# Preparation of queries and keys placed six sixteenths of a tile earlier in every engine's order

## The reference, cut to what matters

```python
def xattn(q, k, v):            # 8 heads of 32 rows each, softmax over the 512 columns
    qk = jnp.einsum('bdm,bdn->bmn', qh, kh) * scale
    ret = jnp.einsum('bmn,bcn->bcm', jax.nn.softmax(qk, axis=-1), vh)

def bitlinear(x, w):
    return jnp.einsum('bsd,fd->bsf', act_quant(x), weight_quant(w))

x = x + xattn(layernorm(x), ctx, ctx)
n = layernorm(x)
x = x + bitlinear(silu(bitlinear(n, W1)), W2)
```

## Time and profile before

| | |
|---|---|
| median of 3 runs | 945.06 us (943.43 to 946.72) |
| profiled execution | 945.5 us, its span 943.5 us |
| busy: TensorE, VectorE | 801.0 us (85%), 801.2 us (85%) |
| busy: ScalarE, GpSimd | 672.2 us (71%), 612.8 us (65%) |
| mean granted TensorE clock | 0.966 of full |
| DMA | 67.97 MB, mean 72 GB/s |

### The profile page before, as it was taken

One profiled execution on the slowest core, in us unless ns is written; L12 is line 12 of the kernel. 1 busy time (PEld: TensorE's weight loads), 2 busy tenths in 40 slices (PEclk: granted clock), 3 DMA queues, 4 the chain that ended last, 5 costly groups with the idle time before them and its releaser, 6 DMA issues.

```text
span 943.5 us, 17275 instructions
## 1 busy us (share of the span) xinstructions
PE 801.0 (85%) x4580; PEld 295.1 (31%) x4580; DVE 801.2 (85%) x1624; ACT 672.2 (71%) x1089; POOL 612.8 (65%) x619
## 2 busy tenths in 40 slices
PE   1658898898899899998899889998899999998875
PEld 0413233333333333332333333332333333333222
DVE  2958999998999899998999899998999999998542
ACT  3577677777777677776777777776777787777753
POOL 4134676776677666775777667775776678775751
PEclk9968899999999999999999999999999999999987
DMA  8540333331233333330333333321333333221000
GB/s 274 173 133 1 68 80 79 80 68 42 60 67 79 79 79 78 67 78 24 66 79 78 79 79 67 78 46 45 79 79 78 79 78 68 57 46 34 23 11 23
DMA packets 49912, 67.97 MB, mean 72 GB/s; under 512 B 6336, under 2 KB 30912, under 8 KB 49344
## 3 DMA queue, kind: packets, MB, share of 16 engines
q1 hardware_dynamic: 49856, 67.39, 29.4%
HBM read 33.55 MB, written 8.39 MB: 44 GB/s over the span
## 4 chain that ended last, share of the span: by engine, by line
PE 45%; DVE 29%; issue 15%; POOL 4%; DMA 2%; ACT 2%; SPq 1%; DVEq 1%; POOLq 0%; ACTq 0%
PE bank_b L937 11%; DVE mx L717 7%; PE pv L906 7%; PE mxp L896 7%; DVE late L791 6%; PE st L886 6%; DVE hmx L796 3%; PE bank_a L975 3%; PE bank_a L927 3%; PE bank_b L975 3%; POOL late L496 2%; DVE sm L770 2%; DVE cparts L722 2%; DMA qs<-ql 1%; PE bank_a L945 1%
## 5 line engine op out<-in xcount | busy, mean ns | idle before, releaser
L469 POOL TENSOR_TENSOR probs<-probs 128x512 f32<-128x512 f32 x256 | 328.4, 1299 | 150.3 <-PE pv L906 99.5
L717 DVE TENSOR_REDUCE mx<-mxp 128x1 f32<-128x512 f32 x512 | 338.5, 681 | 69.5 <-PE mxp L896 54.6
L555 ACT ACTIVATE probs<-st,sm 128x512 f32<-128x512 f32 x512 | 343.0, 685 | 55.7 <-PE st L886 53.3
L896 PE MATMUL mxp<-ks,qs 96*128 96x512 f16 x512 | 203.3, 398 | 52.7 <-DMA qs<-ql 25.0
L886 PE MATMUL st<-qs,ks 98*128 98x512 f16 x512 | 200.0, 392 | 6.4 <-DMA qs<-crow 4.3
L906 PE MATMUL pv<-probs,vt 128*32 128x512 f32 x1024 | 145.2, 640 | 0.0
L937 PE MATMUL bank_b<-w2t,late 128*128 128x512 f16 x512 | 135.4, 389 | 2.6 <-ACT late L587 2.6
L886 PEld LDWEIGHTS st<-qs,ks 98*128 98x128 f16 x512 | 50.3, 98 | 149.5 <-ACT probs L555 78.9
L896 PEld LDWEIGHTS mxp<-ks,qs 96*128 96x128 f16 x512 | 53.9, 105 | 126.0 <-DVE mx L717 58.0
L796 DVE TENSOR_REDUCE hmx<-late 128x1 f32<-128x512 f32 x128 | 84.6, 682 | 2.2
L618 ACT ACTIVATE late<-bank_a,sm 128x512 f32<-128x512 f32 x64 | 44.0, 687 | 59.3 <-PE bank_a L975 59.3
(11 more groups left out here) (92 smaller groups left out, 1034.7 us busy)
## 6 DMA issues: line engine op xcount, KB each, us to landing
xs<-x SPq DMA_DIRECT2D x32, 256.0 KB, 3.8
cs<-ctx SPq DMA_DIRECT2D x32, 256.0 KB, 3.8
ks<-kh SPq DMA_DIRECT2D x64, 128.0 KB, 3.4
qs<-qh SPq DMA_DIRECT2D x64, 128.0 KB, 3.8
xr<-x SPq DMA_DIRECT2D x32, 256.0 KB, 3.4
out<-late SPq DMA_DIRECT2D x32, 256.0 KB, 2.0
probs<-w SPq DMA_DIRECT2D x4, 1024.0 KB, 8.4
ks<-kl SPq DMA_DIRECT2D x32, 128.0 KB, 3.2
```

The lines of the kernel that those rows point to most:

```text
L469: pool.tensor_tensor(probs[:, 2 * pair, h, :], probs[:, 2 * pair, h, :], probs[:, 2 * pair + 1, h, :], ALU.add).then_inc(sum_done, 1)
L555: act.activation(probs[:, c, h, :], st[u % 2][:, :], ACT.Exp, scale=sm1[:, r, ESC:ESC + 1]).then_inc(exp_done, 1)
L717: dve.reduce_max(mx[:, slot.ring(off), NC * h + c:NC * h + c + 1], mxp[m % 2][:, :], axis=AX.X).then_inc(max_done, 1)
L896: pe.matmul(mxp[m % 2][:, :], qs[0:3 * DH, r, h, c * P:(c + 1) * P], ks[0:3 * DH, r, h, :], start=True, stop=True).then_inc(mx_done, 1)
```

## The change

Eleven entries of the plan are made smaller by six: `stats_x`, `aggregate`, `moments`, `rstd`, `key_rsqrt`, `xn`, `qh`, `kh`, `key_scale_b`, `kl` and `ql`. `key_squares`, `key_norm` and `key_scale` stay where they are. The lists in `ORDER` stay too. The constant rows wait for a semaphore value two steps higher, because two more steps of the second tile now stand ahead of them on GpSimd.

```diff
-    stats_x=[-34],
-    aggregate=[-33],
-    rstd=[-31],
-    xn=[-29],
+    stats_x=[-40],
+    aggregate=[-39],
+    rstd=[-37],
+    xn=[-35],
...
-    kh=[-28],
-    qh=[-29],
-    kl=[-27],
-    ql=[-27],
+    kh=[-34],
+    qh=[-35],
+    kl=[-33],
+    ql=[-33],
...
-    key_scale_b=[-28],
-    moments=[-32],
+    key_scale_b=[-34],
+    moments=[-38],
...
-    key_rsqrt=[-30],
+    key_rsqrt=[-36],
...
             def ones_rows(k):

-                pool.wait_ge(x_k_operands, Q_LOW)
+                pool.wait_ge(x_k_operands, Q_LOW + K_SCALE)
```

## The result

| | before | after |
|---|---|---|
| median of the runs, us | 944.24 (941.33 to 946.72, 4 runs) | 1008.44 (1007.45 to 1010.68, 4 runs) |
| ratio, 95% interval | 1 | 1.0684 (1.0647 to 1.0721) |
| span of the profiled execution, us | 943.5 | 1005.9 |
| mean granted TensorE clock in it | 0.966 | 0.949 |

A forecast was written before the change was run, and what follows sets the result against it. The prediction took a feed-forward chain across VectorE, GpSimd and TensorE to set each tile's time: 945.5 us plus 28 x 2.0 = 56 plus 4 for the start gave 1005.5, range asked for 976 to 1028, its own 994 to 1018.

The forecast's parts named there:

- (a): TensorE's first maximum: its 0.56 us a tile wait for the stacking DMAs goes, but was covered: 0, at best -0.3.
- (b): Unit 5 on VectorE: attend product starts ahead of GpSimd's pair sum; token maximum 0.55 us earlier, bounds 0 and 0.8.
- (c): Units 10 to 12: moments and two GpSimd power steps ahead of the quantise, 1.2 us later, +0.65 after the 0.55 credit.
- rival 4: Faster: pair sums move forward by more than the power steps cost, -18 us, 927 us; chance 3%.
- (d): Units 13 and 14 on ScalarE: both casts ahead of the first tanh, which goes from 725.37 to 727.3 us.
- (e): Unit 15 on VectorE: key's low half, held, puts the second gate off by 2.4 us; +2.0 a tile at the transposes.
- The start: Second tile's preparation: constant rows' memset delays its casts and ScalarE's weight sums; +4 us, bounds 0 and +6.
- Rival 1: Unit 15: key step isn't held, +1.3 us a tile, 985.5 us; chance 17%.
- rival 3: More than the sum: attend product stays held (2.6 a tile, 1022 us), or TensorE gets the lower clock more often; 14%.

The follow-up runs named there:

- Experiment 7: Kernel before, with the key's low half alone one unit later (unit 6, behind the attend product): 990.32 us, ratio 1.0494.
- experiment 1: Changed kernel, with the moments and both power steps one unit earlier, ahead of the token scales: 968.35 us, ratio 1.0222 to the kernel before.
- experiment 3: Kernel before, with only statistics, moments and the two power steps six units earlier, and the changed wait of the constant rows: 977.37 us, ratio 1.0327.
- experiment 8: Kernel before, with the preparation earlier but steps placed apart (power steps before the reciprocal, query's cast behind first tanh, key's low half in unit 13): 927.79 us, ratio 0.9849.
- Experiment 4: Changed kernel, with the query's cast one unit later, behind the first tanh: 977.92 us, ratio 1.0331 to the kernel before.
- Experiment 2: Changed kernel, with the key's low half alone put back to unit 5 of the next lap: 985.85 us, ratio 1.041 to the kernel before.
- experiment 5: Changed kernel, with both the query's and the key's cast behind the first tanh: 978.54 us, ratio 1.0376 to the kernel before.
- experiment 6: Changed kernel, with the constant rows' memset at the start three units later and its wait changed: 1004.01 us, ratio 1.0654 to the kernel before.
- experiment 9: Kernel with every step placed apart (927.79 us), with the key's low half alone put back to unit 15 before the second gate: 932.57 us, ratio 0.988 to the kernel before.

## Why the prediction held, and where it was off

The predicted time, 1005.5, is 0.3% from the 1008.44 measured, and the interval, foretold as 28.7, is 28.77. Point by point:

- **(a), the stack.** Right: TensorE's wait is gone but for the first tile, and it was worth nothing that can be seen. Experiment 7 shows how thin its cover was: of 2.1 us of wait a tile some 1.2 come through.
- **(b), the token maximum 0.55 earlier.** Right in size. From the transposes of the hidden tokens to L770 it was 10.92 before and is 10.38 after (801.75 - 791.37). The attend product takes 0.69 as said. One detail fell: the prediction let both small parts of the maxima escape the pair sum. Now the first (L722, 1.22) is held instead of the second (L727, 0.18), since the sum starts just ahead of it. The time is the same, because the sum itself ends 0.55 earlier.
- **(c), power steps ahead of the quantise.** Right: 1.64 - 0.37 = +1.27 for +1.2, and with (b) +0.74 for +0.65. Experiments 1 and 3 put it at 1.40 and 1.23 a tile (the first with the stretches at half clock), the largest part of the change. It is the place where a rival's condition can be seen, too: "it decides if the moments were done before the token scales" was rival 4's, and experiments 1 and 8 make it true. The first took back 40 us, the second came to 927.8, where rival 4 had 927; but 8 also moves the casts and the key step, so this is no proof of that sum.
- **(d), the casts ahead of the tanh.** Right: the tanh comes 1.04 later behind the quantise, +1.8 in all for +1.9. Of the 1.04, the first gate takes on 0.70 (809.04 - 804.29 = 4.75 behind the quantise, for 4.05); the rest is the slack that the prediction named (tanh's end to gate, 0.45 before and 0.11 after). Experiment 4 gives 1.05 a tile back by one cast of 0.62 us, because the key step is held for less as well.
- **(e), the key step held behind the first gate.** Right in the sum: the second gate is 12.36 - 4.29 = 8.07 behind the quantise where it was 6.39 (728.85 - 722.46), +1.68, and with the 0.74 in front +2.4, as said. The transposes follow 28.28 after those of the tile before (791.37 to 819.65) for 26.20, +2.08 for +2.0. Experiment 2 ties both holds to this step. The Trainium skill, "SBUF — State Buffer", section "Who interferes with whom", has issue order decide who blocks; here GpSimd's query step starts 0.24 ahead of the key step and holds it, while GpSimd's query step in experiment 5 starts behind the key step and is itself held (1.60); the rows agree with the rule. Rival 1, the key step free in unit 15, falls with the 1.46 us median, and the first half of rival 3, the attend product still held, with its median of 0.69.
- **The start.** Under-sized: +7.0 at the first quantise against +4, of which the end gave 1.1 back. The memset is as predicted (L828 at 32.63 for 32.3, and experiment 6 takes it away), but it explains 4.1 to 4.5. The prediction stopped at the weight sums. The other 2.5 arise between 61 us and the first quantise, where the first tiles already run in the slowed order; that this makes them was not shown.
- **Rival 3's second half, the clock.** It was kept apart from the forecast, in a case of 14%, and a part of it came along with the forecast: eighteen stretches at the lower level for three. By the estimate above that is about 3 us of the 56.7 of the intervals, so the waits alone made about 54 of the 56 foretold.
- **The loop's ends.** The prediction took no notice of them. Over the five of them the interval grew by 1.3 us in the mean (30.2 for 28.9), inside a pass by 2.2 (28.5 for 26.2), and in the last three, outside the loop, by 2.6 (28.3 for 25.7). That the sum meets the measurement within 3 us, while the start was 3 us short, the clock was put at nothing and the loop's ends grew less than 2.0, is in part luck.

What stays open: why VectorE's pause behind the loop's branch is 3.5 to 3.6 us in experiment 8 and 2.7 to 3.0 before, and what of the shorter edge of experiment 9 is the pause, what the clock.

## What to carry to other kernels

Before a group of steps is shifted as a whole, look at each new neighbour: here eleven cheap steps fell in front of three instructions of one chain (the quantise, the first tanh, the second gate), each putting it off by 1.0 to 1.3 us, and together they cost 6.8%. Nearly the same early shift, with eight of the eleven steps placed anew by one to six units, made the kernel 1.5% faster, so here the neighbours in each engine's order decided, not how early the work was. A 1 us VectorE or GpSimd instruction on large SBUF operands was best costed here by the end of what the other engine runs at that moment, and a step that is freed of a hold can pass the hold to its successor.

## What the runs showed of the hardware that was not expected

- The hold goes both ways and down a queue: GpSimd's residual took 1.72 us behind a held key step (experiment 7), and its query step 1.60 instead of 1.16 (experiment 5). A tiny VectorE cast of 128x16 took 1.22 us beside a pair sum, and 0.17 without.
- A held VectorE instruction of 128x512 ended 0.54 to 0.55 us after the GpSimd instruction that held it, in every such pair of rows shown here (the query step to 811.29, the pair sums to 704.31, 730.97 and 724.38, and the earlier trace rows). The held ones of 128x16 ended 0.03 to 0.04 after it (801.61 for 801.58, 721.28 for 721.24 in the earlier trace rows). The cost of a hold can be worked out from that.
- VectorE pauses behind its branch at the end of each pass of the loop, for 2.7 to 3.0 us in the kernel before and 3.5 to 3.6 in experiment 8, without a wait that the profile shows. A half-clock stretch of TensorE (3.4 or 6.8 us) follows at three of the five loop's ends before and at four of five in experiment 8. Before, an interval across a loop's end is 2.7 us longer than one inside a pass (28.9 for 26.2), which is 0.7 us a tile with four tiles to a pass; in experiment 8 it is 4.5 (29.9 for 25.4), or 1.1 a tile.
